# Separate step tables for the feed-forward products of the iterations that have no output projection

## The reference, cut to what matters

```python
xn = _layernorm(x)                                  # x: (4, 1024, 512) float32
q, k, v = heads(xn @ Wq.T), heads(xn @ Wk.T), heads(xn @ Wv.T)   # 16 heads of 32
probs = softmax(where(causal, q @ k.T / sqrt(32), min))
attn = (probs @ v).reshape(B, S, D) @ Wo.T
gate = silu((xn @ fp8(gate_w)) * gate_scale)        # 512 -> 1536
up = (xn @ fp8(up_w)) * up_scale
ffn = ((gate * up) @ fp8(down_w)) * down_scale      # 1536 -> 512
out = x + attn + ffn
```

## Time and profile before

| what | value |
| --- | --- |
| median of three runs | 1330.88 us (1330.05 to 1332.48) |
| the profiled execution, its own time | 1335.85 us |
| its span, first to last instruction | 1334.1 us |
| mean granted TensorE clock | 0.982 of full speed |
| PE busy | 1253.1 us, 94% of the span |
| DVE, ACT, POOL busy | 81%, 67%, 65% |
| costliest group on PE | the gate and up products (L1488), 204 us each |

### The profile page before, as it was taken

One profiled execution on the slowest core, in us unless ns is written; L12 is line 12 of the kernel. 1 busy time (PEld: TensorE's weight loads), 2 busy tenths in 40 slices (PEclk: granted clock), 3 DMA queues, 4 the chain that ended last, 5 costly groups with the idle time before them and its releaser, 6 DMA issues.

```text
span 1334.1 us, 32685 instructions
## 1 busy us (share of the span) xinstructions
PE 1253.1 (94%) x11812; PEld 829.4 (62%) x11813; DVE 1076.6 (81%) x2752; ACT 895.9 (67%) x1527; POOL 871.5 (65%) x1016
## 2 busy tenths in 40 slices
PE   4999999997898999999999999999999999999987
PEld 2444444344776667676767676677767676676754
DVE  7777778777888888888888798988888888888753
ACT  3322223225878787788878787888878787888841
POOL 1322222204777777787888788878878888888753
PEclk8999999997999999999999999999999999999999
DMA  7489899664555554567656675756675666756441
GB/s 255 116 240 255 238 237 231 180 169 111 110 121 126 118 128 93 129 116 164 120 138 138 119 159 122 160 108 148 121 155 120 139 141 126 157 120 155 81 91 64
DMA packets 419152, 193.98 MB, mean 145 GB/s; under 512 B 330800, under 2 KB 388144, under 8 KB 418992
## 3 DMA queue, kind: packets, MB, share of 16 engines
q1 hardware_dynamic: 397328, 174.84, 57.9%
q10 hardware_dynamic: 21664, 17.05, 4.6%
HBM read 72.89 MB, written 42.21 MB: 86 GB/s over the span
## 4 chain that ended last, share of the span: by engine, by line
PE 33%; POOL 16%; ACT 8%; DVE 7%; issue 6%; DMA 4%; SPq 2%; ACTq 0%; DVEq 0%
PE bank L1488 12%; POOL row L1169 8%; PE bank L1502 8%; PE bank L1464 5%; DMA xt<-xn_parts 3%; POOL fuse L1151 3%; PE pair L206 3%; PE pair L1426 3%; ACT probs L1216 2%; SPq L1073 2%; ACT row L1240 2%; ACT fuse L1255 2%; POOL probs L1035 2%; PE pair L1519 2%; DVE row_top L1359 2%
## 5 line engine op out<-in xcount | busy, mean ns | idle before, releaser
L1226 ACT ACTIVATE p<-pair,s_exp 128x512 f32<-128x512 f32 (+1 forms) x384 | 243.3, 634 | 161.2 <-PE pair L1426 159.7
L1169 POOL TENSOR_TENSOR row<-row 128x896 f16<-128x896 f32 (+1 forms) x128 | 256.1, 2010 | 11.5 <-ACT row L1240 11.4
L1216 ACT CAST probs<-p 128x512 f16<-128x512 f32 (+1 forms) x384 | 214.7, 559 | 14.4 <-POOL p L1163 13.5
L1035 POOL TENSOR_TENSOR probs<-p,probs 128x512 f16<-128x512 f32 x192 | 221.2, 1156 | 0.2
L1488 PE MATMUL bank<-xt,wg 128*128 128x256 f16 x1536 | 204.1, 277 | 7.2 <-DMA xt<-xn_parts 4.7
L1488 PE MATMUL bank<-xt,wu 128*128 128x256 f16 x1536 | 204.0, 277 | 0.0
L1502 PE MATMUL bank<-wd,fuse 128*128 128x512 f16 x768 | 190.6, 378 | 0.9 <-DVE ff_out L1340 0.9
L1163 POOL TENSOR_SCALAR_AFFINE_SELECT p<-p 128x128 f32<-128x128 f32 (+1 forms) x256 | 108.5, 428 | 110.6 <-ACT p L1226 108.6
L1359 DVE TENSOR_REDUCE row_top<-pair 128x1 f32<-128x896 f32 (+1 forms) x128 | 147.2, 1150 | 24.0 <-PE pair L1444 24.0
L1488 PEld LDWEIGHTS bank<-xt,wg 128*128 128x128 f16 x1536 | 141.8, 99 | 36.8 <-DMA xt<-xn_parts 11.0
L1488 PEld LDWEIGHTS bank<-xt,wu 128*128 128x128 f16 x1536 | 144.3, 99 | 23.0 <-issue 0.2
(11 more groups left out here) (153 smaller groups left out, 2160.0 us busy)
## 6 DMA issues: line engine op xcount, KB each, us to landing
q_st<-q_parts SPq DMA_DIRECT2D x192, 64.0 KB, 2.6
k_st<-k_parts SPq DMA_DIRECT2D x192, 64.0 KB, 2.0
v_parts<-res SPq DMA_DIRECT2D x8, 1056.0 KB, 6.5
v_sb<-v_parts SPq DMA_DIRECT2D x64, 132.0 KB, 2.2
xn_parts<-x_t SPq DMA_DIRECT2D x16, 512.0 KB, 7.6
q_parts<-qk_st SPq DMA_DIRECT2D x32, 256.0 KB, 4.5
k_parts<-qk_st SPq DMA_DIRECT2D x32, 256.0 KB, 4.1
xt<-xn_parts SPq DMA_DIRECT2D x16, 512.0 KB, 4.6
```

Of the source, the lines that this page charges most:

```text
L1035: ops.tensor_tensor(probs[n % 2][:, LO, at], p32[e % RING][:, 0:UNIT_WIDTH[u]], probs[n % 2][:, HI, at], ALU.subtract).then_inc(signal, 1)
L1169: nc.gpsimd.tensor_tensor(row16[r][:, w:2 * w], row32[r][:, :], row16[r][:, 0:w], ALU.subtract).then_inc(row_lo, 1)
L1216: nc.scalar.copy(probs[n % 2][:, HI, u * 512:u * 512 + w], p32[e % RING][:, 0:w]).then_inc(p_hi, 1)
L1226: nc.scalar.activation(p32[e % RING][:, 0:w], st_bank[u % 2][:, 0:w], ACT.Exp, scale=s_exp[:, :]).then_inc(exp_done, 1)
```

## The change

`GATE_STEP` and `UP_STEP` become tuples of three tables: the first for iteration 0, the second for iterations 1 to 3, the third, with the old numbers, for iterations 4 to 15. `kind(it)` chooses. The steps of tanh, swiglu and fuse are derived from `UP_STEP` for each table as before. The work itself is the same: no instruction is added or removed on any engine, only places in the order change.

```diff
--- before.py
+++ after.py
@@ -137,24 +137,41 @@
              9: [(1, 0), (1, 1)], 10: [(1, 2)], 11: [(1, 3)], 12: [(1, 4)], 13: [(1, 5)]}
 DOWN_PIECES = 6
 ADD_DOWN_STEP = {5: 0, 14: 1}
-GATE_STEP = {4: 0, 6: 1, 8: 2, 14: 3, 16: 4, 18: 5, 19: 6, 23: 7, 25: 8, 27: 9, 31: 10, 33: 11}
-UP_STEP = {5: 0, 7: 1, 13: 2, 15: 3, 17: 4, 18: 5, 22: 6, 24: 7, 26: 8, 27: 9, 31: 10, 34: 11}
-TANH_STEP = {k + 1: f for k, f in UP_STEP.items()}
-SWIGLU_STEP = {k + 2: f for k, f in UP_STEP.items()}
-
-FUSE_STEP = {**{k + 3: f // 2 for k, f in UP_STEP.items() if f > 1 and f % 2 == 1}, 15: 0}
+GATE_STEP = ({0: 0, 2: 1, 6: 2, 9: 3, 11: 4, 15: 5, 18: 6, 20: 7, 24: 8, 27: 9, 29: 10, 33: 11},
+             {4: 0, 6: 1, 8: 2, 14: 3, 16: 4, 18: 5, 20: 6, 22: 7, 25: 8, 27: 9, 29: 10, 32: 11},
+             {4: 0, 6: 1, 8: 2, 14: 3, 16: 4, 18: 5, 19: 6, 23: 7, 25: 8, 27: 9, 31: 10, 33: 11})
+UP_STEP = ({1: 0, 4: 1, 7: 2, 10: 3, 13: 4, 16: 5, 19: 6, 22: 7, 25: 8, 28: 9, 31: 10, 34: 11},
+           {5: 0, 7: 1, 13: 2, 15: 3, 17: 4, 19: 5, 21: 6, 23: 7, 26: 8, 28: 9, 30: 10, 33: 11},
+           {5: 0, 7: 1, 13: 2, 15: 3, 17: 4, 18: 5, 22: 6, 24: 7, 26: 8, 27: 9, 31: 10, 34: 11})
+
+
+def behind_up(steps):
+
+    return tuple({k + steps: f for k, f in table.items()} for table in UP_STEP)
+
+
+TANH_STEP = behind_up(1)
+SWIGLU_STEP = behind_up(2)
+
+FUSE_STEP = tuple({k: f // 2 for k, f in table.items() if f % 2 == 1} for table in behind_up(3))
+FUSE_STEP = (FUSE_STEP[0],) + tuple({15 if p == 0 else k: p for k, p in table.items()} for table in FUSE_STEP[1:])
 SPLIT_STEP = {12: 0, 20: 1}
 PROJ_STEP = {20: [(0, 0)], 21: [(0, 1)], 22: [(0, 2)], 28: [(1, 0)], 29: [(1, 1)], 30: [(1, 2)]}
 PROJ_PIECES = 3
 ADD_OUT_STEP = {23: 0, 31: 1}
 
 
-def at_step(table, it, k):
-
-
-    found = [(table[k], it)] if k in table else []
-    if k + STEPS in table and it > 0:
-        found.append((table[k + STEPS], it - 1))
+def kind(it):
+
+    return min(it, 1) if it < LAG else 2
+
+
+def at_step(tables, it, k):
+
+
+    found = [(tables[kind(it)][k], it)] if k in tables[kind(it)] else []
+    if it > 0 and k + STEPS in tables[kind(it - 1)]:
+        found.append((tables[kind(it - 1)][k + STEPS], it - 1))
     return found
 
 
@@ -1564,10 +1581,10 @@
 
                                     pe.wait_ge(mt_copied, 4 * it + 1 + i)
                                 down(i, piece, it - 1)
-                        if k in GATE_STEP:
-                            feed_forward(0, GATE_STEP[k], it)
-                        if k in UP_STEP:
-                            feed_forward(1, UP_STEP[k], it)
+                        for f, t in at_step(GATE_STEP, it, k):
+                            feed_forward(0, f, t)
+                        for f, t in at_step(UP_STEP, it, k):
+                            feed_forward(1, f, t)
                         if with_out:
                             for i, piece in PROJ_STEP.get(k, ()):
                                 if piece == 0:
```

## The result

The change made the kernel slower: 1353.49 us median (1350.79 to 1357.71, four runs) against 1331.18 before, a ratio of 1.0164 (95% interval 1.0141 to 1.0187). I had forecast 1342.4, in a range of 1331 to 1349. So the sign was right and the size half of what came: +22.3 us against +11.5, outside the range.

The account below looks back on a forecast made before the run. PE looked like the bound, but DVE and ACT set the first halves of touched heads. Iteration 0 (7.2 - 1.3 + 2.6 = 8.5) plus iterations 1 to 3 (3.0) gave +11.5 us: 1342.4 us, range 1331 to 1349.

Parts of the forecast that it names:

- The stall and head 0: Iteration 0, head 0: G(0), moved to step 0, waits 4.2 us for xt; the head ends 7.2 us later.
- The tanh chain: Changed heads: tanh behind row 0's exponential delays swiglu and row 1's maximum; first halves (E0's scores to maxima unit 2) 9.2-9.8 us.
- Iterations from 4 on: Iterations 4 to 15: no effect, since their steps are the old ones and PE's work hides everything else.
- iteration 0, heads 1 to 3: 14.5 us a head, -1.3 us in all, plus 2.6 us for two falls of the clock.
- iterations 1 to 3, heads 2: Row 1's maximum starts 1.1 us later, the second half has one product fewer: +0.2 us each.
- iterations 1 to 3, heads 3: -0.6 us each from 14.3 us against 14.9, then +1.4 us each for a fall in the second half.
- The clock: Gathered PE waits ahead of unit 2 drop it: +2.6 us in iteration 0, +1.4 in each head 3 of iterations 1 to 3.
- third rival: Low clock in each of the changed heads of iterations 0 to 3: +18.5 us, 1349.4 us; chance 0.10.
- long single gaps: Rival: low clock only behind the longest gaps, in head 0 and the three head 3s: +8.9 us, 1339.8; chance 0.10.
- 6.9 - 0.9 = 6.0: Head 2 of iterations 1 to 3: second half, from maxima unit 2 on, has three products where it had four.
- 5.1 in head 3: Head 3 of iterations 1 to 3: the second half, from maxima unit 2 on, takes 5.1 us.

Follow-up runs that it names:

- e3: The changed kernel with ACT doing the tanh ahead of row 0's exponential in step u = 2; 1339.40 us, ratio 1.0061 to the kernel before.
- e4: The changed kernel with DVE taking the maximum of row 1 ahead of the swiglu in step u = 3; 1341.54 us, ratio 1.0083 to the kernel before.
- e6: The changed kernel with U(7) and U(11) of iterations 1 to 3 back in steps 24 and 34; 1355.11 us, ratio 1.0168 to the kernel before.
- e14: The kernel before with twelve unused matmuls in each of six heads to hold the clock, load of xt unmoved; 1325.75 us, ratio 0.9967.
- e12: The kernel before with the load of xt earlier in SyncE's queue and twelve unused matmuls to hold the clock; 1317.52 us, ratio 0.9906.
- e1: The changed kernel with its new table in iteration 0 only, old steps in iterations 1 to 3; 1345.78 us, ratio 1.0104 to the kernel before.

## Why the prediction was wrong

Right, by its own steps:

- *The stall and head 0.* Forecast 7.2 us later, measured 21.2 against 13.9: 7.3. The stall was 4.23 us for 4.2.
- *The tanh chain.* Forecast first halves of 9.4, 9.8 and 9.2 us; measured 9.35 in head 1 of iteration 0, and 9.84 and 9.35 in heads 2 and 3 of iteration 1. `e3` and `e4` show the cause. Heads 2 and 3 of iteration 0 took 9.95 and 10.39, for the reason in the last point below.
- *Iterations from 4 on* kept their steps and nearly their times.

By place, in the two profiled executions, in us:

| place | forecast | measured |
| --- | --- | --- |
| iteration 0, head 0 | +7.2 | +7.3 |
| iteration 0, heads 1 to 3 | +1.3 | +5.0 |
| iterations 1 to 3, heads 2 | +0.6 | +6.1 |
| iterations 1 to 3, heads 3 | +2.4 | +6.9 |
| iterations 2 and 3, heads 0 | 0 | +1.3 |
| iterations 4 to 15 | 0 | +2.5 |
| ahead of `attend` | 0 | -7.2 |
| sum | +11.5 | +21.9 |

The mechanisms of the forecast were there. Two terms of its sum were too small, each by some 7 us in this execution:

- *The clock* (forecast 2.6 + 3 x 1.4 = 6.8, measured about 14: 3 x 1.6, then 1.2 and 1.3 in heads 2, and 6.7 in heads 3). I had counted two falls in iteration 0's heads 1 to 3 at 1.3 us, and one in each of iterations 1 to 3 at 1.4. PE's idle time ahead of unit 2 was forecast well (2.6 us in iteration 0, measured 2.63; 3.7 in head 3, measured 3.32); what the clock made of it was not. There were three in iteration 0 at 1.6. In iterations 1 to 3 every head 3 and two of three heads 2 ran low, and the low stretch was twice as long in two of the heads 3. In head 3 of iteration 1 it lasted almost 6 us from the end of the wait:

```profile
426.80:430.10 3.30, 0.01 (x1) 0.00 (x0) 3.16 (x11) 3.14 (x5) 3.30 (x3) 0.83 0.81 233
430.10:436.00 5.90, 5.87 (x48) 4.26 (x49) 3.12 (x10) 1.68 (x3) 1.62 (x3) 0.52 0.02 5
```

  The second halves of these heads took 8.15, 7.16 and 8.20 us, and 5.6 in `e3` where the same order on PE kept its clock. My third rival, low clock in each of these heads, gave 1349.4 and was the nearest. In head 2 of iteration 2 the clock fell with gaps of 0.33, 0.79 and 1.49 us ahead of it. The Trainium skill, "TensorE: Matmul & The Clock Gate", section "Why this matters for your kernels", warns only of long single gaps; the measurement decides against taking that as the whole rule. Nor do the gaps alone decide: head 2 of iteration 1 had the same ones and kept the full clock.

- *What a swiglu holds up behind itself* (forecast nothing: "6.9 - 0.9 = 6.0" in head 2, 5.1 in head 3, and "Heads 0 and 1 ...: nothing"; measured about 7: 3 x 0.9 in heads 2, 3 x 0.5 in heads 3, 1.3 in heads 0, 1.5 in iteration 0). One product fewer did not shorten head 2: its second half measured 6.92 us at full clock, and PE waited 0.75 us in it for DVE ahead of unit 7. Head 3's took 5.6 at full clock, not 5.1. I had followed only what a swiglu does ahead of unit 2, not what it does behind it. Likewise the swiglu of f = 11, now in u = 8, stood ahead of the normalisation and made the next head 0 take 16.2 us, not 15.6. Heads 2 and 3 of iteration 0 waited 0.44 and 0.88 us in their first halves for the normalisation too. `e6` shows the limit of this point: with the two up products moved back these waits went, but about as much came elsewhere.

What stays open: when the clock falls. Code that is the same fell in one execution and not in another, and I can only say what one fall cost. The executions of one kernel differed by 2 to 9 us in most sets (by 16 in one set of 19). How much of that is the clock and how much the varying start of `attend` was not separated.

## What to carry to other kernels

In a program whose order is fixed step by step, a step moved on one engine moves a piece on every engine behind it: follow each of them to the next shared wait, and also past it. Work moved into a wait is only free if its successors do not stand ahead of what ends the wait. Where TensorE waits, price the clock as well as the wait; a few unused matmuls there can pay. One profile shows the falls of one execution only, so compare medians before you trust a sum read from it.

## What was not expected of the hardware

- Twelve small matmuls a head, in six heads of 64 (0, 1 and 3 of iteration 0, 3 of iterations 1 to 3), made the kernel before 4 us faster (`e14`, ratio 0.9967, 0.9950 to 0.9983). In the profiles of `e14` and `e12` the granted clock stayed at 1.00 from the second head to the end of iteration 3, where it had fallen five times in the profile of the kernel before.
- One fall cost 1.5 us in a head of 14: the same code at both levels in one execution (`e3`).
- Heads 3 of `e14` took 13.6 us in iterations 1 to 3, as in `e1`, yet PE waited for xt at G(0) only from iteration 4 on. Why the load was in time there is not settled.
